# Who scales the softmax numerators: two query tiles in one VectorE product

## The reference

```python
h = tok(x); h = concat([h, txt])                    # 32 x 273 x 128
# attention, on layernorm(h)
logits = einsum('bhid,bhjd->bhij', q, k) * scale
logits = einsum('bhij,gh->bgij', logits, w_pre)     # mix heads
attn   = softmax(logits, axis=-1)                   # exp(x - max) / sum of the row
attn   = einsum('bhij,gh->bgij', attn, w_post)      # mix heads again
out    = einsum('bhij,bhjd->bhid', attn, v)
h = h + out @ w_out.T + b_out
h = h + ffn(layernorm(h))                           # top 2 of 8 experts, gelu
```

## Time and profile before

| | us |
|---|---|
| median of 3 runs | 1492.24 (1491.61 to 1493.64) |
| the profiled execution | 1497.27 |
| its span | 1495.4 |
| PE busy in the span | 1242.3 |
| ACT busy | 1021.6 |
| DVE busy | 949.0 |
| POOL busy | 852.1 |

### The profile page before, as it was taken

One profiled execution on the slowest core, in us unless ns is written; L12 is line 12 of the kernel. 1 busy time (PEld: TensorE's weight loads), 2 busy tenths in 40 slices (PEclk: granted clock), 3 DMA queues, 4 the chain that ended last, 5 costly groups with the idle time before them and its releaser, 6 DMA issues.

```text
span 1495.4 us, 34349 instructions
## 1 busy us (share of the span) xinstructions
PE 1242.3 (83%) x8194; PEld 1064.1 (71%) x8195; DVE 949.0 (63%) x3348; ACT 1021.6 (68%) x3007; POOL 852.1 (57%) x1653
## 2 busy tenths in 40 slices
PE   5899999999999999999999999998199999995000
PEld 4677777777777777777777777777099999994000
DVE  4776667767677676677666776663245454444887
ACT  2687878778777878787787877874055555553665
POOL 2135545555555655556555555553546666665998
PEclk9999999999999999999999999997589999998555
DMA  5001110101101011010111010100222222221554
GB/s 227 18 27 39 48 31 30 34 30 51 34 30 34 30 49 36 30 34 30 39 42 34 30 34 30 35 18 17 61 68 76 76 79 74 77 78 54 156 158 128
DMA packets 69455, 82.29 MB, mean 55 GB/s; under 512 B 11626, under 2 KB 59725, under 8 KB 68898
## 3 DMA queue, kind: packets, MB, share of 16 engines
q1 hardware_dynamic: 57216, 57.16, 13.2%
q0 software_dynamic: 11328, 19.07, 4.1%
q10 hardware_dynamic: 866, 5.55, 0.9%
HBM read 52.08 MB, written 30.65 MB: 55 GB/s over the span
## 4 chain that ended last, share of the span: by engine, by line
PE 41%; POOL 21%; issue 18%; DVE 12%; ACT 4%; POOLq 1%; DMA 1%; DVEq 1%; SPq 1%; ACTq 0%
PE PS L1411 9%; PE PS L1174 6%; PE PS L1258 5%; PE PS L1220 4%; PE PS L1398 3%; PE PS L1399 2%; PE PS L1400 2%; POOL rs L626 2%; DVE nmax L923 2%; POOL nr L507 2%; DVE VP L890 2%; POOL cf L525 2%; DVE bst L845 2%; POOL EK L495 2%; DVE sl L982 2%
## 5 line engine op out<-in xcount | busy, mean ns | idle before, releaser
L1220 PE MATMUL PS<-kT,qs 128*128 128x273 f32 x1024 | 280.1, 396 | 2.2 <-ACT E L668 1.8
L1258 PE MATMUL PS<-AT,VP 128*128 128x273 f32 x1024 | 278.4, 394 | 0.0
L923 DVE TENSOR_REDUCE nmax<-PS 128x2 f32<-128x546 f32 (+1 forms) x288 | 206.1, 715 | 73.1 <-PE PS L1220 73.1
L668 ACT ACTIVATE E<-PS,nmax 128x273 f32<-128x273 f32 x512 | 243.4, 483 | 11.8 <-DVE nmax L923 9.1
L556 POOL DMA_INDIRECT dram_routed<-xr,slu x192 | 189.5, 987 | 64.8 <-issue 64.8
L1220 PEld LDWEIGHTS PS<-kT,qs 128*128 128x128 f32 x1024 | 184.1, 190 | 36.1 <-issue 2.9
L607 POOL DMA_INDIRECT dram_results<-arena,du x152 | 166.3, 1094 | 64.2 <-issue 54.6
L695 ACT COPY AT<-PS 128x512 f32<-128x512 f32 x256 | 151.0, 590 | 67.8 <-PE PS L1238 65.5
L1258 PEld LDWEIGHTS PS<-AT,VP 128*128 128x128 f32 x1024 | 175.0, 191 | 20.4
L1238 PEld LDWEIGHTS PS<-small,E 128*128 128x128 f32 x1024 | 125.7, 140 | 46.8 <-ACT ATR L702 16.3
L1238 PE MATMUL PS<-small,E 128*128 128x128 f32 x1024 | 155.8, 274 | 3.0 <-ACT ATR L702 0.6
(11 more groups left out here) (187 smaller groups left out, 2745.5 us busy)
## 6 DMA issues: line engine op xcount, KB each, us to landing
arena<-in_x SPq DMA_DIRECT2D x32, 588.0 KB, 3.8
arena<-dram_routed SPq DMA_DIRECT2D x76, 144.0 KB
stage<-dram_results SPq DMA_DIRECT2D x32, 196.0 KB
dram_h<-H SPq DMA_DIRECT2D x32, 147.0 KB
w1hl<-dram_h SPq DMA_DIRECT2D x32, 147.0 KB
out<-w1hl SPq DMA_DIRECT2D x32, 98.0 KB
dram_routed<-xr,slu POOLq DMA_INDIRECT x192, 2.3
stage<-dram_results SPq DMA_DIRECT2D x32, 77.0 KB
```

Source lines behind the costliest of these rows:

```text
L668: nc.scalar.activation(bank, PS[0:rows, 2 * ((par + u) % 2) + t, 0:N], ACT.Exp, bias=nmax[0:rows, u, t:t + 1], accum_out=esum[0:rows, u, t ...
L923: v.tensor_reduce(nmax[0:rows, u], PS[0:rows, b0:b0 + 2, 0:N], AX.X, ALU.max, negate=True).then_inc(S["max"], 1)
L1220: last = mm(PS[0:rows, 2 * ((par + u) % 2) + t, 0:N], q, kT[:, par, 0:N], start=True, stop=True)
L1258: last = mm(acc, VP[:, par, g, c, :], AT[:, g, c, :], start=(g == 0 and c == 0), stop=False)
```

## The change

DVE's `head_probs` turns from a product of one tile (t = 0) with a column of reciprocals into one product of both tiles with both columns, broadcast along the keys. ACT's `scaled` is left with head 0, the packed left-over queries. The semaphore `probs_act` counts only head 0 now, so that the waits on it change their numbers, and PE's transposes of heads 1 to 8 wait for `probs` alone.

```diff
             def scaled(i, u):
 
-                act.wait_ge(S["recip"], NU * i + u + 1)
                 if u == 0:
+                    act.wait_ge(S["recip"], NU * i + u + 1)
                     for t in range(2):
                         last = nc.scalar.activation(ER[:, t, 0:N], ER[:, t, 0:N], ACT.Copy,
                                                     scale=rsum[0:RM, 0, t:t + 1])
-                else:
-                    own_tile = E[:, (u - 1) % EB, 1, 0:MQ]
-                    last = nc.scalar.activation(own_tile, own_tile, ACT.Copy, scale=rsum[:, u, 1:2])
-                last.then_inc(S["probs_act"], 1)
+                    last.then_inc(S["probs_act"], 1)
...
             def head_probs(i, u):
 
                 dve.wait_ge(S["recip"], NU * i + u + 1)
-                tile = E[:, (u - 1) % EB, 0, 0:MQ]
-                v.tensor_scalar(tile, tile, rsum[:, u, 0:1], None, ALU.mult).then_inc(S["probs"], 1)
+                tiles = E[:, (u - 1) % EB, :, 0:MQ]
+                v.tensor_tensor(tiles, tiles, rsum[:, u].unsqueeze(2).broadcast_to([128, 2, MQ]), ALU.mult
+                                ).then_inc(S["probs"], 1)
 
             def own_keys(i, par):
 
-                dve.wait_ge(S["probs_act"], NU * i + 1)
+                dve.wait_ge(S["probs_act"], i + 1)
...
-                pe.wait_ge(S["probs_act"], NU * i + u + 1)
                 if u > 0:
                     pe.wait_ge(S["probs"], NH * i + u)
+                else:
+                    pe.wait_ge(S["probs_act"], i + 1)
```

## The result

The changed kernel took 1570.28 us in the median of 4 runs (1562.46 to 1571.75), the kernel before 1492.14 (1491.61 to 1493.64, 4 runs beside it): 1.0511 times as long, 95% interval 1.0475 to 1.0548. So it is 5.1% slower, where 3.0% was forecast, and above the forecast range of 1508 to 1551 us.

A forecast was written before the change was run, and what follows sets the result against it. It took a once-per-image loop through PE, DVE and POOL as the bound. Per image -0.17 (ACT) + 0.84 (DVE) + 0.28 + 0.28 + 0.32 (POOL) = +1.55 us, over 29 images 45 us: 1537 us, range 1508 to 1551.

The forecast's parts named there:

- the loop: PE's scores, DVE to the residual's statistics, POOL to tokb, DVE to VR, which releases PE; closes once per image.
- The rival in which PE's order is the bound: PE at 94% busy sets the pace, so each image is 0.40 us shorter: 1480 us; chance 0.06.
- the one without a hold: POOL isn't hindered by the new DVE product: 1512 us; chance 0.22, with partial hindrance between the two.
- slower still: Transposes or the ring of four E tiles begin to wait for late products: above 1551 us; chance 0.08.
- waits for xr and VR: PE's waits for ACT's xr in step 0 and DVE's VR: together about 2 us more per image.
- Heads 4 and 8: Their DVE products lie on the loop and take longer than the old scalings: +0.25 us each per image.
- the lower bound: No hindrance on POOL at all: 0.67 us per image, 19 us, so 1512 us.
- Head 3: Step 3: reciprocals no longer wait for ACT (-0.17), longer DVE product (+0.34), held POOL power of norm1 (net +0.28 us).
- The gain from ACT: In step 3 head 3's reciprocals no longer wait for ACT: 0.17 us per image gained on the loop.
- What it adds on POOL: The product holds back three POOL operations per image: power L456 net +0.28, power L507 +0.28, EK +0.32 us.
- the EK at 615.04: POOL operation starting 0.19 us after head 7's scaling; forecast to be held by the product, +0.32 us per image.
- the bound of 1551 us: Upper bound: every product at +0.34 and one more EK held, 2.03 us per image, 59 us.

The follow-up runs named there:

- late_scalar: Kernel before, with DVE's old scaling moved to the end of each step except steps 3 and 8; 1471.96 us, ratio 0.9861.
- two_scalars: Changed kernel, with DVE's one product written as two scalings, each a tile times a column; 1515.41 us, ratio 1.0153 to the kernel before.
- act_kept_busy: Changed kernel, with ACT doing eight activations of the old size per image on other data; 1571.22 us, ratio 1.0528 to the kernel before.
- max_first_6: Changed kernel, with DVE taking the maximum ahead of the product in step 6; 1542.09 us, ratio 1.0332 to the kernel before.
- max_first_67: Changed kernel, with DVE taking the maximum ahead of the product in steps 6 and 7; 1535.61 us, ratio 1.0291 to the kernel before.
- paced_8: Kernel before, with a DVE reduction of 640 constant elements, result unused, ahead of head 8's scaling only; 1523.98 us, ratio 1.0202.

## Why the prediction was wrong

The direction, the loop and the mechanism were right; the size was not.

**The loop** held: what was added to DVE and POOL on it came out in the period. The rival in which PE's order is the bound is out (`late_scalar` leaves PE's order as it was and is faster), and so is the one without a hold (`two_scalars`). The rival "slower still" has the time, but not its reason: PE waits for none of the new products. Wrong was where PE's idle time would lie. Its waits for xr and VR were to grow by about 2 us per image together; that for xr grew by 0.6 (34.7 us over 28, before 17.8 over 28) and that for VR not at all, and new are 1.2 us for ACT's ATR in step 8 and 0.6 for its xnT in step 6 (32.3 and 17.0 over 28). The one for oT is 0.8, as forecast.

**The product**: 0.69 us for the forecast 0.68, next instruction 0.61 behind it. Heads 4 and 8 cost 0.25 each, as forecast. The price of DVE's length with no POOL operation of the three held is that of `two_scalars`, 0.66 us per image, where the lower bound had 0.67.

**Head 3**: forecast -0.17 + 0.34 + 0.28 = 0.45, measured 0.31: DVE's `xn` comes 1.30 us after the start of the power (647.88, 649.18) where it came 0.99 after it (603.34, 604.33). The hold was there: 0.37 on the power, which starts 0.18 us behind the product and not the 0.09 of the forecast. The gain from ACT was not a gain (`act_kept_busy`).

**The step that failed** is the one under "What it adds on POOL". In steps 6 to 8 it is 1.5 us per image, where 0.60 was forecast. The prediction measured the hold on a power 0.10 us behind a product, looked for POOL operations that stand 0.1 to 0.3 us behind a scaling, and took those. It left out the ones that start in the same instant: L505, released by the same statistics; L517; and L527. The trace of before shows two of them plainly: L505 at 608.90 beside a scaling at 608.91, L527 at 614.89 beside one at 614.85. Instead the text priced L507 (unchanged at 0.85) and the EK at 615.04, which only inherit what the operation ahead of them was held. (That EK is of head 7; the prediction's last part calls it head 6's.) And it took for L505's neighbour the rest of a hold (0.28), where a start together pays the whole of it (0.55). Measured: L505 +0.55, L517 +0.50, L527 +0.50. With them the sum is 0.31 + 0.25 + 0.55 + 0.50 + 0.50 + 0.25 = 2.36, and EK of head 7 is 0.05 shorter than before (0.24, was 0.29); the trace has 2.31.

L517 stood 0.23 us ahead of the scaling before the change, so it seemed safe. But L505's hold pushed POOL back 0.55 us and head 6's product moved only by the 0.24 that came after head 5, so that L517 stands 0.05 us behind it; `max_first_6` takes the first away and the second goes with it. That chain is the reason that the bound of 1551 us was too low: it took in one more hindrance, and none that makes the next.

**The clock** was in no case of the prediction: 8 us of the 78, five images in which TensorE ran at 1.2 GHz for 3.4 us. They are counted in the one execution that was traced; another, the one of 1562.46 us, had a mean granted clock of 0.936 over the whole run, against 0.933 in the traced one, so it probably had fewer of them.

## What to carry to other kernels

Before a scaling on DVE becomes a product of two SBUF operands, list for each of its executions what GpSimd starts while it streams, first of all what the same event releases: two operations that start together do so in every period, and the later one pays the whole stream. Price the hold by the product's elements, then shift everything behind it by the hold and look again for operations that now meet. Look at the order of the instructions first: moving the old scaling behind work that others wait for gave 1.4% with no new operation.

## What the runs showed of the hardware

**The hold between DVE and POOL.** A POOL operation that starts up to 0.01 us ahead of a DVE product of two SBUF operands, or while it streams, does its own work only some 0.55 us after the product's start at 512 elements and some 0.28 at 256; at 0.09 us ahead it isn't held. That POOL's operation is small (three columns) does not help, nor that the second operand is a broadcast of two values. A DVE product that reads one operand from PSUM did not hold POOL: in the kernel before, the rope product of 294 columns lies over POOL's L512, which keeps its 0.19.

```profile
610.34 0.51 DVE L880 SCALAR_TENSOR_TENSOR rsn<-PS,small,cosT 128x294 f32<-128x294 f32 x1
...
610.54 0.19 POOL L512 TENSOR_TENSOR nr<-nm,mone 98x3 f32<-98x3 f32 x1
```

The Trainium skill (SBUF — State Buffer, "Who interferes with whom") has this as a lock on a shared port, held for the whole instruction by whoever comes first. The rows agree where the product comes first, and in `max_first_67`, where DVE is the one that waits. They do not agree for POOL's powers. By that rule a product that started 0.23 us into the power L507 would have waited for its end; it took 0.68 us, its usual length (`max_first_6`). Why a power is no hindrance stays open.

**A scaling can be held too.** In `two_scalars` the first DVE scaling of head 6 took 1.51 us in place of 0.35. It starts in POOL's power L517, and EK and the rope sum follow without a gap:

```profile
623.85 0.85 POOL L517 TENSOR_TENSOR rr<-tv,mhalf 98x3 f32<-98x3 f32 x1
...
624.32 1.51 DVE L906 TENSOR_SCALAR E<-E,rsum 128x256 f32<-128x256 f32 x1
...
624.67 0.24 POOL L495 TENSOR_TENSOR EK<-E,rsum 128x34 f32<-128x34 f32 x1
...
624.87 0.81 POOL L479 TENSOR_TENSOR qT<-rc,rsn 128x294 f32<-128x294 f32 x1
```

It ends 0.15 us after the rope sum (L479). POOL's lengths are the old ones, so here only DVE waits, and in its slack. The power is not likely to have begun it: scalings that started 0.22 us into it in the kernel before, and products that started 0.23 and 0.40 us into powers in `max_first_6`, were not longer. The rope sum alone does hold a scaling: that of head 7 in the same run starts 0.23 us into one, with no power beside it, takes 0.74 us, and also ends 0.15 us after it. But head 6's scaling started 0.55 us before its rope sum, and how it came to wait that long stays open.

**TensorE's clock.** In all six runs with images at half the clock, PE's longest wait for xr was 1.6 or 1.7 us, in every second image, and 29 of 72 such waits were followed by 3.4 us at 1.2 GHz, which began 0.6 to 1.7 us behind the wait; in the eight other profiles it was 1.4 us at most, and none had such an image between 100 and 985 us (behind that, where the last images run out, some have). `paced_8` made this wait 1.6 us where it was 1.0 (and 1.0 in the images between, where it was 0.4), and left PE's other waits as they were; its images are also 0.6 us longer than before. Waits of 1.1 to 1.2 us for oT, 31 of them in the kernel before, do nothing of the kind. Why some of the long waits are followed by it and others not stays open, and with it the cause.
